# A one-core vision-tower kernel: first three hidden chunks in three banks, merged row loads, reordered set-up loads, an earlier store

## The reference, cut to what matters

```python
h = tok(x, scharr)                          # gray picture, 3x3 edge filter in two directions, mean of |.|
h = layernorm(h + attn(h, Wq, bq, Wk, bk, Wv, bv))   # causal softmax attention, 8 pictures of 256 x 256
h = layernorm(h + ffn(h, Wr, W1, W2))       # top-1 of 8 experts
# ffn: idx = argmax(softmax(t @ Wr)); pos = rank of the token within its expert; kept = pos < cap (320)
#      ein[e] = the kept rows of expert e;  h = relu(ein @ W1[e]);  eout = h @ W2[e]
#      out row = eout * pmax if kept, else the token itself ("plain" row)
```

## Time and profile before

| what | value |
|---|---|
| median of three runs | 249.90 us |
| profiled execution | 249.95 us |
| its span, first to last instruction | 248.20 us |
| busy: TensorE, VectorE, ScalarE, GpSimd | 94%, 74%, 61%, 40% |
| chain that ended last, share by engine | PE 80, issue 4, POOL 4, DVE 4, ACT 3, DMA 3 (%) |

### The profile page before, as it was taken

The page is one execution under the profiler, slowest core; times in us unless marked ns, Lnnn a source line. Parts: engine busy times, 40 slices in busy tenths (PEclk is TensorE's granted clock), DMA queues, the critical chain, the costliest instruction groups (busy, mean ns, idle before and its releaser), DMA issues.

```text
span 248.2 us, 4995 instructions
## 1 busy us (share of the span) xinstructions
PE 232.4 (94%) x1673; PEld 222.6 (90%) x1673; DVE 184.4 (74%) x557; ACT 151.4 (61%) x354; POOL 98.5 (40%) x169
## 2 busy tenths in 40 slices
PE   6899999999999999878999999999999999999940
PEld 5699999999999998756999999999999999999940
DVE  4885697978879799985656797749977678779550
ACT  5335467777778787465665577656775757656100
POOL 7000236484846658458200020156261332613672
PEclk9999999999999999999999999999999999999995
DMA  4939283255697120201899709156092460100100
GB/s 148 285 114 321 87 261 101 73 181 201 197 371 242 42 73 12 83 0 44 230 361 339 263 0 339 44 191 237 0 319 75 152 218 3 47 0 24 35 4 0
DMA packets 28378, 35.48 MB, mean 143 GB/s; under 512 B 2780, under 2 KB 25291, under 8 KB 28354
## 3 DMA queue, kind: packets, MB, share of 16 engines
q1 hardware_dynamic: 26144, 31.71, 39.4%
q0 software_dynamic: 1792, 3.47, 3.9%
q10 hardware_dynamic: 418, 0.00, 0.1%
HBM read 26.97 MB, written 9.47 MB: 147 GB/s over the span
## 4 chain that ended last, share of the span: by engine, by line
PE 80%; issue 4%; POOL 4%; DVE 4%; ACT 3%; DMA 3%; POOLq 1%; DVEq 0%; ACTq 0%
PE bank L1279 15%; PE bank L1281 15%; PE bank L1280 15%; PE bank L1350 14%; PE bank L1367 5%; PE bank L1404 4%; POOL out_dram L572 3%; DMA bqc<-in_L_attn_bq_dram 3%; PE bank L1529 2%; PE bank L1420 2%; PE bank L1579 2%; PE bank L1378 2%; PE bank L1421 1%; PE bank L1422 1%; POOL yrstd L596 1%
## 5 line engine op out<-in xcount | busy, mean ns | idle before, releaser
L1196 DVE SCALAR_TENSOR_TENSOR h_lo<-bank,h_hi 128x320 fp32r<-128x320 f32 x58 | 28.3, 489 | 27.3 <-ACT h_hi L816 24.5
L816 ACT ACTIVATE h_hi<-bank 128x320 fp32r<-128x320 f32 x58 | 25.3, 436 | 35.4 <-PE bank L1281 34.9
L572 POOL DMA_INDIRECT out_dram<-tokens_mem,images x24 | 28.0, 1167 | 37.9 <-ACT tokens_mem L833 17.1
L1279 PE MATMUL bank<-einT_hi,w_hi 128*128 128x320 f32 x128 | 40.6, 317 | 0.6 <-DVE einT_lo L1188 0.3
L1281 PE MATMUL bank<-einT_hi,w_lo 128*128 128x320 f32 x128 | 39.6, 309 | 0.0
L1280 PE MATMUL bank<-einT_lo,w_hi 128*128 128x320 f32 x128 | 39.5, 309 | 0.0
L946 DVE TENSOR_TENSOR w_lo<-w_raw,w_hi 128x1024 fp32r<-128x1024 f32 x32 | 38.9, 1214 | 0.0
L1279 PE MATMUL bank<-h_hi,w_hi 128*128 128x320 f32 x112 | 35.3, 315 | 0.1
L1280 PE MATMUL bank<-h_lo,w_hi 128*128 128x320 f32 x112 | 34.7, 310 | 0.0
L1281 PE MATMUL bank<-h_hi,w_lo 128*128 128x320 f32 x112 | 34.6, 309 | 0.0
L744 ACT ACTIVATE w_hi<-w_raw 128x1024 fp32r<-128x1024 f32 x32 | 33.7, 1053 | 0.0
(11 more groups left out here) (230 smaller groups left out, 578.2 us busy)
## 6 DMA issues: line engine op xcount, KB each, us to landing
w_raw<-in_L_ffn_W_dram SPq DMA_DIRECT2D x16, 1024.0 KB
images<-in_x_dram SPq DMA_DIRECT2D x7, 768.0 KB
dispatched<-blank SPq DMA_DIRECT2D x4, 645.0 KB, 9.1
images<-dispatched SPq DMA_DIRECT2D x9, 258.0 KB, 7.0
out_dram<-lone SPq DMA_DIRECT2D x8, 256.0 KB, 7.0
images<-in_x_dram SPq DMA_DIRECT2D x2, 384.0 KB, 6.0
images<-dispatched SPq DMA_DIRECT2D x9, 64.5 KB, 7.0
out_dram<-tokens_mem,images POOLq DMA_INDIRECT x24
```

The source lines that it names most:

```text
L572: pool.indirect_dma_start(out_rows, bass.IndirectOffsetOnAxis(ap=ein[0:n, e, j, D + 1:D + 2].bitcast(U32), axis=0), z[0:n, e % 2, j, :], N ...
L816: act.activation(hidden_halves(n)[0], bank[n % 2][:, 0:CAP], ACT.Relu).then_inc(h_hi_ready, 1)
L1196: dve.scalar_tensor_tensor(lo, bank[n % 2][:, 0:CAP], 0.0, hi.bitcast(F32), ALU.max, ALU.subtract).then_inc(h_ready, 1)
L1279: pe.matmul(to, ah, bh, start=first, stop=False)
```

## The change

Nothing in the arithmetic changes. The diff, cut to what the text speaks of:

```diff
 SyncE
             def load_rows(e):
+                if 0 < e < E - 1:
+                    sp.dma_start(ein[:, e, :, :],
+                                 dispatched[e * CAP:e * CAP + NS * P].rearrange("(j p) r -> p j r", p=P)
+                                 ).then_inc(ein_in[e], 16)
+                    return
+            sp.dma_start(taps[:, :], bass.AP(scharr.tensor, 0, [[0, 1], [1, TAP_COLS]])).then_inc(taps_in, 16)
             sp.dma_start(wq[:, :, :], ...)
-                if e == 4:
+                if e == 3:
                     store_lone(L)
 GpSimd
-                pool.memset(ein[CAP - full * P:P, :, full, :], 0.0).then_inc(spare_rows_ready, 1)
+                pool.memset(ein[CAP - full * P:P, 0:E:E - 1, full, :], 0.0).then_inc(spare_rows_ready, 1)
 ScalarE
-            def band_high():
-                act.wait_ge(band_ready, 2)
-                act.activation(band_hi[:, :, :, :], band[:, :, :, :], ACT.Copy).then_inc(band_hi_ready, 1)
+            def band_high(dx):
+                act.wait_ge(band_ready, 2 * (dx + 1))
+                act.activation(band_hi[:, dx], band[:, dx], ACT.Copy).then_inc(band_hi_ready, 1)
-            act.dma_start(taps[:, :], bass.AP(scharr.tensor, 0, [[0, 1], [1, TAP_COLS]])).then_inc(taps_in, 16)
             act.dma_start(wk[:, :, D:D + 1], ...)
+            act.wait_ge(row_ready, 1)
+            act.activation(still_row[:, :], one_row[:, :], ACT.Copy).then_inc(still_row_ready, 1)
-            for dx in range(TAPS):
+            for dx in range(1, TAPS):
                 for f in range(2):
                     ...
-            band_high()
+            for dx in range(TAPS):
+                band_high(dx)
             for c in range(DC):
                 edges(0, c)
-            gray_high(1)
             tokens_high(0)
             ...
                 project_keys(i)
+                if i == 0:
+                    gray_high(1)
-                act.activation(hidden_halves(n)[0], bank[n % 2][:, 0:CAP], ACT.Relu).then_inc(h_hi_ready, 1)
+                act.activation(hidden_halves(n)[0], hidden_bank(n)[:, 0:CAP], ACT.Relu).then_inc(h_hi_ready, 1)
-                    if e == 2 and j == 6:
+                    if e == 1 and j == 6:
                         norm_lone(L)
 VectorE
             def make_band(dx):
-                dve.wait_ge(part_ready, dx + 1)
+                if dx == 0:
+                    for f in range(2):
+                        tap = f * TAPS * TAPS
+                        step(dve.tensor_scalar(band[:, 0, f, :], tap_mask[:, 0], half_taps[:, tap:tap + 1], None,
+                                               ALU.mult))
+                    settle()
+                else:
+                    dve.wait_ge(part_ready, dx)
-            make_gray(1)
             for c in range(DC):
                 tokens(0, c)
-            gray_low(1)
             tokens_low(0)
             ...                                # the side columns of the value weights, setup_ev 2
+            make_gray(1)
             ...
                 keys_low(i)
+                if i == 0:
+                    gray_low(1)
 TensorE
+        def hidden_bank(n):
+            return bank[(0, 6, 2, 1)[n] if n < 4 else n % 2]
-            keep_warm(9)
+            keep_warm(6)
             setup_keys()
             setup_biases()
-            setup_values()
-            for t in range(3):
+            for s in range(SC):
+                for c in range(DC):
+                    convolve(0, c, (0,), (s,))
+                if s == 0:
+                    setup_values()
+            for t in (1, 2):
                 for c in range(DC):
                     convolve(0, c, (t,))
-            def hidden(e, j):
+            def hidden(e, j, parts=range(DC)):
-                if n >= 2:
+                if n >= 4:
                     pe.wait_ge(h_ready, n - 1)
-                for k in range(DC):
+                for k in parts:
                     ...
+            for k in range(DC):
+                for j in range(3):
+                    hidden(0, j, (k,))
             for e in range(E):
                 for j in range(FC):
-                    hidden(e, j)
+                    if e or j > 2:
+                        hidden(e, j)
```

More of the change, by code:

```diff
@@ L85, in vit_tower_kernel @@
         one_row = sb("one_row", [1, P])
+        still_row = sb("still_row", [1, P])
         half_taps = sb("half_taps", [P, TAP_COLS])
@@ L229, in vit_tower_kernel @@
         late_z_ready = sem("late_z_ready")
+        still_row_ready = sem("still_row_ready")
         spare_rows_ready = sem("spare_rows_ready")
@@ L896, in make_band @@
                                                        band[:, dx, f, :], ALU.mult, ALU.add)
-                        if dx < TAPS - 1 or dy < TAPS - 1:
+                        if dy < TAPS - 1:
                             step(ins)
@@ L924, in _ @@
             gray_low(0)
-            dve.wait_ge(band_hi_ready, 1)
+            dve.wait_ge(band_hi_ready, TAPS)
             dve.tensor_tensor(band_lo[:, :, :, :], band[:, :, :, :], band_hi[:, :, :, :].bitcast(F32), ALU.subtract
@@ L1195, in hidden @@
                 hi, lo = hidden_halves(n)
-                dve.scalar_tensor_tensor(lo, bank[n % 2][:, 0:CAP], 0.0, hi.bitcast(F32), ALU.max, ALU.subtract
+                dve.scalar_tensor_tensor(lo, hidden_bank(n)[:, 0:CAP], 0.0, hi.bitcast(F32), ALU.max, ALU.subtract
                                          ).then_inc(h_ready, 1)
@@ L1329, in setup_gate, with convolve @@
                 ins.then_inc(setup_mm, 1)
-            def convolve(b, c, terms=range(3)):
+            def convolve(b, c, terms=range(3), rows=range(SC)):
                 if 0 in terms and b >= 1:
@@ L1343, in convolve @@
                         pe.wait_ge(band_lo_ready, 1)
-                    for s in range(SC):
+                    for s in rows:
                         if b == c == t == 0:
                             pe.wait_ge(gray_hi_ready if s else first_gray_ready, 1)
-                            pe.wait_ge(band_hi_ready, 1)
+                            pe.wait_ge(band_hi_ready, TAPS)
                         for dx in range(TAPS):
@@ L1353, in convolve @@
                                             start=first, stop=last, skip_group_check=True)
-                if 2 in terms:
+                if 2 in terms and SC - 1 in rows:
                     ins.then_inc(conv_done, 1)
@@ L1524, in ein_t @@
             def ein_t(e):
-                pe.wait_ge(ein_in[e], 32)
+                pe.wait_ge(ein_in[e], 16 if e < E - 1 else 32)
                 pe.wait_ge(einT_ready, DC * e)
@@ L1541, in hidden @@
                     w = slice(k * F + j * P, k * F + (j + 1) * P)
-                    ins = product(bank[n % 2][:, 0:CAP], (w_hi[:, e % 2, w], w_lo[:, e % 2, w]),
+                    ins = product(hidden_bank(n)[:, 0:CAP], (w_hi[:, e % 2, w], w_lo[:, e % 2, w]),
                                   (einT_hi[:, e % 2, k, :], einT_lo[:, e % 2, k, :]), k == 0, k == DC - 1)
-                ins.then_inc(h_done, 1)
+                if DC - 1 in parts:
+                    ins.then_inc(h_done, 1)
             def wait_hidden(e, j):
```

## The result

The changed kernel took 248.33 us in the median of twelve runs (247.62 to 249.07), the kernel before 249.54 us in the same session; the ratio is 0.9947, 95% interval 0.9924 to 0.9970. That is 1.2 us faster. Ratios with an interval leave out the executions that lie more than 1.5% above the fastest of their kernel.

A forecast was written before the change was run, and what follows sets the result against it. TensorE, 80% of the chain, was taken as the bound, so edits pay only where it waits or its work shortens. Terms -0.55 - 0.2 + 0.34 - 0.28 = -0.69 gave 249.95 - 0.69 - 0.05 = 249.2 us, range 248.5 to 250.8.

The forecast's parts named there:

- taps on SyncE's queue, key bias first: Start: key bias issued 0.58 us earlier, latencies unchanged, next step at 9.1 instead of 9.69; -0.55 us, bounds -1.2 and +0.15.
- rival 3: Start gains its full bound, -1.2 us in place of -0.55: total 248.6 us; chance 0.10.
- token step: Picture 0's tokens: halves and set-up event 0.2 us sooner once picture 1's gray is moved; -0.2 us, bounds -0.4 and 0.
- Rival 1: Start: with fewer warmers TensorE's clock stays low through the keys, +1.3 in place of -0.55; about 250.8 us; chance 0.28.
- Rival 2: Start: Wk lands at 7.56 us or later and the start gains nothing; total 249.8 us; chance 0.18.
- Filter bands: Start: VectorE makes the first two parts itself; bands and gray stay covered by 1 us or more; 0.
- merged rows: Experts: one DMA for an expert's rows saves six issues, reads a fifth more bytes; 0, bounds -0.1 and +0.3.
- memset: A memset a quarter as long, on an engine the chain doesn't name there; 0.
- Picture 1's gray moved: ScalarE's and VectorE's gray work no longer precedes picture 0's token halves, which start sooner; -0.2 us, bounds -0.4 and 0.
- Three banks: Expert 0: chunk 0 complete 0.34 us later, pushing back VectorE's third low piece and `expert_out`; +0.34 us, bounds +0.2 and +0.5.
- Rival 4: Expert 0: three banks pay as written, 1 us goes instead of 0.34 coming; total 247.9 us; chance 0.03.
- Plain rows: Last picture's plain rows one expert earlier, ending GpSimd's store wait near 150 and expert 3's hole; -0.28 us, bounds -0.29 and 0.

The follow-up runs named there:

- piece_first: Changed kernel with VectorE's third low piece of expert 0's weights made ahead of `h_lo` of chunk 0: 247.68 us, ratio 0.9915.
- best_prewarm: Fastest version (third low piece early, two full chunks first) plus one matmul on constants ahead of the wait for the taps: 247.50 us, ratio 0.9915.

## Why the prediction was right or wrong

**The step that failed: taps on SyncE's queue, key bias first.** It was set at -0.55 and measured -1.03 in the profiled pair, and about -1.1 is left for it by the medians (below). Its mechanism (slot, bias first, `bqc` with it) was right; the size was off in two places that partly offset each other. "With unchanged latencies" was wrong: the bias took 2.8 to 3.1 us in the profiled executions of all eight kernels that have it first, where the old order showed 4.6, 4.6, 5.1, 5.6, 5.9 and 5.9, and Wk 3.4 to 3.6 in the seven with the taps on SyncE's queue, against 3.6 to 5.6. The keys started at 5.34 and not at 7.1. Against that, the keys took 3.48 us and not 2.0, because their larger part ran at the lower clock: the keys begin 2.04 us sooner, and from their start to that of the biases it is 3.32 us instead of 2.31 (keys 1.51 longer, less 0.33 of waiting for `bqc` and some 0.17 that lies in the modelled ends), sum -1.03. The forecast made one execution's landings into a property of the code. The rows it had in hand spoke for the other value: a bias of 1 KB that takes as long as a load of 256 KB suggests that it stands behind something, and the text gave that as the reason for rival 3. The other term that it took from the same execution, a start at 9.69 behind two waits, was a draw too: 8.83, 9.07 and 10.93 in other executions of that start.

**The range.** Other executions of the changed order start the biases at 7.58, 7.68 and 7.84: with the same start the clock rose at 6.28, 6.53 and 6.86 us there and at 8.53 in the profiled execution of the changed kernel. With the other terms taken from the traces (-0.28, +0.18, +0.30, -0.28), the medians' 1.2 us leave about -1.1 for the start, which lies inside that step's own bound of -1.2. But rival 3 was given a chance of 0.10, and the low end of the range was laid only 0.1 under its 248.6, so that a start at its bound and a token step a little over its value were already outside.

**Rival 1, the clock.** Half came true. The keys ran mostly at the lower level, as it said; it gave the sum wrongly because it kept the bias late, with "a gap of near 2 us" behind the matmuls on constants. The condition "it decides from the point where the keys end later than 9.7" was the right one: they ended at 8.8. Where the condition is met, in the two variants with late loads and six matmuls, the low clock is there in the profiled execution, with the biases at 10.19 and 10.64, and in the worst executions the loss is larger than the +1.3 it was given. The sentence "they ran at 2.4" on the earlier trace rows is true of that execution only; another with the same start shows 3.77 us.

**Rival 2, Wk late.** Fell: Wk's latency dropped by 2.0 us and its issue moved by 0.36.

**Filter bands, merged rows, memset: 0.** Held in the profiled execution; none of them was run alone. No wait for them stands in the trace after, and the filter follows the biases without a bracket. The cover of 1 us or more was smaller than the text had it once the start gained more: in `piece_first`, with the biases at 7.68, the filter's first rows waited 0.37 us for ScalarE's high half of the gray picture, and the values came 0.5 us later behind the biases than in the other executions. The merged load, of 387 KB, takes 8.9 us, and no `ein_t` waits for it.

**Picture 1's gray moved: -0.2.** Measured -0.28 between the biases and the values of the profiled pair. Over more executions it is -0.2, as forecast: 9.97 to 10.08 us in five with the old order and the clock up, 9.78 to 9.81 in four with the new one (9.89 in `best_prewarm`, and 10.32 in `piece_first` with the wait named above). No variant had this edit alone.

**Three banks: +0.34.** Measured +0.30 in the changed kernel and alone, with one hole of 1.40 us where 1.5 was expected, ended by the third low piece. This is the part of which the prediction was surest and the one that held best. Rival 4 with it fell in the changed kernel; with VectorE's piece moved, most of the gain that it named (about 1 us) is there: 0.92 at the first `expert_out`, 0.57 at the end.

**Plain rows: -0.28.** Windows 15.39 and 15.68 became 15.40 and 15.39; shown by the trace, not by the time alone.

**What nobody forecast: +0.18.** Between the values of picture 0 and expert 0 part of the gain is given back. One step holds it: from the values of the fourth picture to those of the fifth it is 11.38 to 11.42 us in all seven traces with the picture loop of the kernel before, and 11.58 to 11.63 in all seven with that of the changed kernel, with early loads and with late ones. TensorE's rows have no bracket there, but VectorE's have, between two small instructions of a layer norm that follow each other at once in the kernel before:

```profile
57.28 0.18 DVE L1056 BATCH_NORM_AGGREGATE mv<-stats 128x2 f32<-128x6 f32 x1 [0.21 <-issue]
```

This pause of 0.21 us stands in all seven traces of the changed program and in none of the other seven. Behind it GpSimd's and ScalarE's work and the attention's matmuls begin 0.16 to 0.22 us later against the start of the step. "Issue" means that the profile shows nothing that VectorE waited for, so why this program has the pause there stays open. The two steps behind this one (11.17 to 11.41 us and 11.18 to 11.37) differ as much between executions of one program.

## What to carry to other kernels

Where two loads are late together, ask which of them is made of tiny pieces and what it is issued behind: try it as the first issue of its queue, and put what must come even sooner on another queue. Read latencies of set-up loads from several executions before one of them becomes a term, for one profile is one draw. Matmuls on constants that raise the clock, and the landing of the data behind them, are one choice, not two: shorten the one only when the other is early. And when more banks let TensorE run ahead, move what the first consumer needs to the front of the other engine's list as well; alone the banks cost 0.30 us, and with the piece moved they gave 0.92 at that point and 0.57 at the end.

## What the runs showed of the hardware

- A load of 256 pieces of 4 bytes took 2.8 to 3.1 us when it was first in ScalarE's queue, issued at 0.80 us (eight kernels), and 4.6 to 5.9 us one place later, issued at 1.38 with the 72 bytes of the taps ahead of it and Wk's 256 KB issued on SyncE's queue at 1.24 (six kernels). Whether the place or the order against Wk makes the difference was not separated. The taps, issued behind it at 1.49, landed at 4.7 us instead of 2.1 (one execution). The Trainium skill ("DMA: Bandwidth & Descriptors", section "Issuing engines are not separate DMA queues") says that spreading DMAs over engines saves only the time to initiate them. Here the taps at the head of either queue landed 2.6 us sooner than behind the bias, and only 0.69 us of that is the later issue; on this point the measurement decides.
- When TensorE's clock rises at the start is a matter of the single execution. With six matmuls on constants and the keys right behind them, it rose at 6.28, 6.53, 6.86 and 8.53 us in four executions, and the eight key matmuls took 2.40 to 3.48 us. With nine and a hole of 0.52 us it rose at 7.35 in one execution and at 11.40 in another. With six and a hole of 1.05 or 1.51 us it rose at 18.4 and 11.52. None of the 57 executions with the loads early (taps on SyncE's queue) was more than 1.0 us above its kernel's median; of the 29 of the kernel before in the last session five were 1.7 us or more above theirs (251.57 to 252.60 against 249.81), and how fast the clock rose in those is not on record.
- In these traces the record of the granted clock begins only with the rise, and a window's clock column reads 1.00 ahead of it although the matmuls step at the lower level. At a kernel's start the step between matmuls is the witness to read.
